# Norms, routing and part of the sends of a routed stage put into the last steps of the cross attention before it

## The reference, cut

```python
x = x + jnp.tanh(g_xattn[2]) * _L2_xattn_ref(_layernorm(x, axis=-1), ctx_1024, ctx_1024, ..., 1)
x = x + jnp.tanh(g_ffn[2]) * _L2_ffn_ref(_layernorm(x, axis=-1), L2_ffn_Wr, L2_ffn_W1, L2_ffn_W2)
```

```python
router_logits = x @ Wr.T                     # 2048 rows, 8 experts
routing_weights = jax.nn.softmax(router_logits, axis=-1)
top_w, top_idx = jax.lax.top_k(routing_weights, TOP_K)      # 2
h = jax.nn.silu(jnp.einsum('td,edf->tef', x, W1))           # 512 hidden
y = jnp.einsum('tef,efd->ted', h, W2)
out = jnp.einsum('te,ted->td', comb, y)
```

## Time and profile before

| | us |
|---|---|
| median of 3 runs | 1419.97 |
| lowest and highest | 1415.36, 1420.51 |
| the profiled execution | 1427.67 |
| its span, first to last instruction | 1425.7 |
| TensorE busy | 1133.1 (79%) |
| VectorE busy | 697.3 (49%) |
| ScalarE busy | 614.2 (43%) |
| GpSimd busy | 443.4 (31%) |

### The profile page before, as it was taken

The page is one execution under the profiler, slowest core; times in us unless marked ns, Lnnn a source line. Parts: engine busy times, 40 slices in busy tenths (PEclk is TensorE's granted clock), DMA queues, the critical chain, the costliest instruction groups (busy, mean ns, idle before and its releaser), DMA issues. The chain is left out here.

```text
span 1425.7 us, 26533 instructions
## 1 busy us (share of the span) xinstructions
PE 1133.1 (79%) x8710; PEld 774.7 (54%) x8710; DVE 697.3 (49%) x3353; ACT 614.2 (43%) x1535; POOL 443.4 (31%) x636
## 2 busy tenths in 40 slices
PE   5998885499989999988987963997586999961684
PEld 3676744277745666653434742786452454441573
DVE  4564546133368776534553452111756788754002
ACT  3454453233369766423213230332462666630453
POOL 1674415333406455400002416343010000016343
PEclk8999987699999999999996865799685899975797
DMA  7499131222069920013530021454143222040343
GB/s 203 131 276 234 38 104 38 60 83 81 22 111 135 170 64 2 2 50 81 100 74 1 2 67 46 144 174 136 36 135 111 69 54 71 20 141 25 97 124 93
DMA packets 150262, 128.54 MB, mean 90 GB/s; under 512 B 13193, under 2 KB 126745, under 8 KB 150136
## 3 DMA queue, kind: packets, MB, share of 16 engines
q1 hardware_dynamic: 135256, 107.67, 31.4%
q0 software_dynamic: 7824, 15.47, 3.9%
q10 hardware_dynamic: 7056, 3.81, 1.0%
HBM read 88.91 MB, written 40.85 MB: 91 GB/s over the span
## 5 line engine op out<-in xcount | busy, mean ns | idle before, releaser
L304 POOL TENSOR_TENSOR L_Z<-L_Z,L_mx 128x512 f32<-128x512 f32 x84 | 88.5, 1055 | 271.1 <-DVE L_mx L615 271.1
L3070 DVE CUSTOM_DVE_ANT_0 L3s_masked<-L3s_psS,L3s_trilw 128x512 f32<-128x512 f32 (+3 forms) x256 | 109.1, 487 | 35.0 <-PE L3s_psS L2969 34.5
L863 ACT ACTIVATE L_Z<-L_Z,L_nmx 128x154 f32<-128x154 f32 x256 | 105.1, 414 | 42.0 <-DVE L_nmx L913 41.9
L3041 ACT ACTIVATE L3s_E<-L3s_psT 128x512 f32<-128x512 f32 (+1 forms) x192 | 87.9, 531 | 49.8 <-PE L3s_psT L2982 49.5
L732 POOL TENSOR_TENSOR L_Z<-L_Z,L_rin 128x488 f32<-128x488 f32 x64 | 64.0, 1000 | 111.8 <-DVE L_rin L921 111.8
L615 DVE CUSTOM_DVE_ANT_0 L_Z<-L_psS,L_Z 128x154 f32<-128x154 f32 x256 | 63.4, 313 | 57.6 <-PE L_psS L352 45.9
L774 PE MATMUL L_psS<-L1k_G,L_xnT 128*128 128x462 f32 x192 | 82.4, 525 | 2.8 <-DVE L_nmx L913 1.4
L913 DVE CUSTOM_DVE_ANT_0 L_Z<-L_psS,L_mask 128x154 f32<-128x154 f32 x256 | 67.7, 313 | 11.2 <-PE L_psS L774 10.7
L513 ACT ACTIVATE L_E<-L_psT 128x512 f32<-128x512 f32 x84 | 46.1, 596 | 57.2 <-PE L_psT L365 57.2
L2969 PE MATMUL L3s_psS<-L3s_KS,L3s_QS 72*128 72x512 bf16 (+3 forms) x256 | 55.9, 336 | 11.4 <-PEq L2955 8.5
L931 DVE COPY L_PT<-L_psT 122x512 f32<-122x512 f32 x64 | 43.6, 682 | 40.4 <-PE L_psT L784 39.5
(11 more groups left out here) (543 smaller groups left out, 2857.5 us busy)
## 6 DMA issues: line engine op xcount, KB each, us to landing
L_Z<-in_fside_Bx16xSxS SPq DMA_DIRECT2D x16, 1232.0 KB
L2f_w<-in_L_ffn_W SPq DMA_DIRECT2D x39, 256.0 KB
slotsL<-empty SPq DMA_DIRECT2D x1, 8320.5 KB, 68.4
L1m_cb<-comb_rows SPq DMA_DIRECT2D x8, 1024.0 KB
L3f_w<-in_L_ffn_fc_w SPq DMA_DIRECT2D x32, 256.0 KB
L0f_w<-in_L_ffn_W SPq DMA_DIRECT2D x24, 256.0 KB
q_parts<-L3s_parts SPq DMA_DIRECT2D x12, 384.0 KB, 5.3
L3s_QS<-q_parts SPq DMA_DIRECT2D x16, 288.0 KB
```

Source lines behind the costliest of these rows:

```text
L304: nc.gpsimd.tensor_tensor(Z[:, t % NZ, h, 0:KM_], Z[:, t % NZ, h, 0:KM_], top.broadcast_to([P, HG, KM_]), ALU.subtract).then_inc(z_ready, 1)
L863: last = nc.scalar.activation(Z[:, t % 2, h], Z[:, t % 2, h], ACT.Exp, scale=-1.0, bias=nmx[:, t % 2, h:h + 1], accum_out=sums[:, t % 2, h ...
L3041: nc.scalar.activation(E[:, g.par, h, EO[group[0]]:EO[group[0]] + wd], psT[:, k, 0:wd], ACT.Exp).then_inc(t_free, 1)
L3070: last = nc.vector.tensor_tensor_reduce(masked[:, k, at:at + wd], psS[:, k, at:at + wd], trilw[:, S - wd:S], 1.0, LOW, ALU.add, ALU.max, m ...
```

## The change

- **Chunks** of L2f are now tile i of every batch (`tiles(k)` is `slice(k, NT, TB)`). So chunks 0, 1 and 2 are the uniform tiles, final after t = 2 of the attention, and chunk 3 is the four tiles of its steps t = 3 to 6.
- **The route is made before the attention** and is handed to both stages; its semaphores live on, and `Keys3` and `SelfState` get their memory earlier too. `begin` moves to the attention's start.
- **In the attention at t = 2**, VectorE measures chunks 0 and 1 between the two residuals, and normalises both and measures chunk 2 behind the second. ScalarE takes the two deviations between its exponentials.
- **At t = 3** TensorE turns chunk 0 and 1 in two new fillings of `psT`, and multiplies with the router into spare columns of `psS`, once all maxima are done. VectorE chooses chunk 0 ahead of the residual.
- **At t = 4 and 5** TensorE counts chunk 0 and 1; VectorE places chunk 0 and chooses chunk 1, then places chunk 1 and normalises chunk 2. ScalarE takes the third deviation.
- **GpSimd**, behind its last subtraction, scatters chunk 0 (8 DMAs) and the first tile of chunk 1 (2 DMAs). The other 22 stay in L2f.
- **`Lead2`** keeps chunks 2 and 3.

The core of the diff:

```diff
+            if late:
+                pool.wait_ge(m.wiped, 64)
+                for g, sent in ((0, route.each(0)), (1, route.sent)):
+                    pool.wait_ge(route.slots_ready, g + 1)
+                    pool.wait_ge(route.pay_done, g + 1)
+                    for t in sent:
+                        route.scatter(pool, m.slots["L2"], t)
...
+            def route_logits(k):
+                pe.wait_ge(t_done, slot[("r", k)] + 1)
+                route.logits(pe, k)
...
+                if late and t in (4, 5):
+                    route.positions(pe, t - 4)
...
+                if late and t == 3:
+                    pe.wait_ge(s_done, 4 * NTL)
+                    route_logits(0)
...
+                if late and t == 3:
+                    route_logits(1)
...
+                    if t == 2:
+                        route.deviation(act, 0)
+                        route.deviation(act, 1)
...
+                if late and t == 4:
+                    route.deviation(act, 2)
...
+                    dve.wait_ge(y_done, written[("y", t)] + 1)
+                    route.moments(0, m.X)
+                    route.moments(1, m.X)
                     dve.wait_ge(y_full, written[("y2", t)] + 1)
                     x = by_batch[:, :, 2]
                     nc.vector.scalar_tensor_tensor(x, y, m.gate(c["gate"]), x, ALU.mult, ALU.add).then_inc(y_done, 1)
+                    route.apply(0, m.X)
+                    route.apply(1, m.X)
+                    dve.wait_ge(y_done, written[("y2", t)] + 1)
+                    route.moments(2, m.X)
...
+                if late and t >= 3:
+                    if t in (4, 5):
+                        route.place(t - 4)
+                    if t in (3, 4):
+                        route.choose(t - 3)
+                    if t == 5:
+                        route.apply(2, m.X)
...
     def tiles(self, k):
-        return slice(k * TB, (k + 1) * TB)
+        return slice(k, NT, TB) if self.c["kind"] == "L2" else slice(k * TB, (k + 1) * TB)
...
     def tensor(self, pe):
         route = self.route
-        route.turn(pe, 0)
-        route.logits(pe, 0)
-        for k in range(TB):
-            if k + 1 < TB:
-                route.turn(pe, k + 1)
-                route.logits(pe, k + 1)
-            route.positions(pe, k)
+        route.turn(pe, 2)
+        route.logits(pe, 2)
+        route.turn(pe, 3)
+        route.positions(pe, 2)
+        route.logits(pe, 3)
+        route.positions(pe, 3)
         self.kv.tensor(pe, self.sa)
...
         route, x = self.route, self.m.X
-        route.begin(dve)
+        route.resume(dve)
+        route.moments(3, x)
+        route.choose(2)
+        route.apply(3, x)
+        route.place(2)
         self.kv.vector(dve)
...
-            for g in range(TB):
+            for g in range(1, TB):
                 pool.wait_ge(route.slots_ready, g + 1)
                 pool.wait_ge(route.pay_done, g + 1)
-                for t in range(g * TB, (g + 1) * TB):
...
+                for t in route.each(g):
+                    if g > 1 or t not in route.sent:
+                        route.scatter(pool, slots, t)
```

More of the change, by code:

```diff
@@ L170, in quad_attention @@
 def quad_attention(nc, m, c):
-    nm, late = c["name"], c["late"]
+    nm, late, route = c["name"], c["late"], c.get("route")
     W, DK = 9, 8
@@ L218, in quad_attention @@
                 take(slot, key)
-            for g in (2, 3, 4):
+            for g in (2, 3):
                 take(slot, ("z", t, g))
+            if not late:
+                take(slot, ("z", t, 4))
             for key in extras(t, 1):
                 take(slot, key)
+            if late:
+                take(slot, ("z", t, 4))
         if 0 <= t - 2 < NTL:
@@ L257, in quad_attention @@
         v_clear, vr_full = sem("v_clear"), sem("vr_full")
+        if late:
+            spare = HG * P - 3 * S2
+            assert spare >= (TB + 1) * route.E
+            route.banks(None, psS[:, 3, 3 * S2:512], psS[:, 2, 3 * S2:512])
+            route.sent = route.each(1)[:1]
         block = ctx.enter_context(nc.Block())
@@ L463, in _ @@
                     turn_scores(t, 3)
+                if late:
+                    for key in extras(t, 1):
+                        extra(key)
                 if last_:
@@ L467, in _ @@
                     turn_scores(t, 4)
-                for key in extras(t, 1):
-                    extra(key)
+                if late and t == 3:
+                    route_logits(1)
+                if not late:
+                    for key in extras(t, 1):
+                        extra(key)
         @block.scalar
@@ L1283, in turn, with turn_rows @@
     def turn(self, pe, k):
+        if k > self.first:
+            pe.wait_ge(self.t_done, k - self.first)
+        self.turn_rows(pe, k, self.bank_t).then_inc(self.t_full, 1)
+    def turn_rows(self, pe, k, bank):
         pe.wait_ge(self.x_ready, k + 1)
-        if k >= 1:
-            pe.wait_ge(self.t_done, k)
-        for i in range(TB):
-            last = pe.transpose(self.bank_t[:, i * P:(i + 1) * P], self.pay[:, 0, k * TB + i, 0:D], self.m.ident)
-        last.then_inc(self.t_full, 1)
+        for i, t in enumerate(self.each(k)):
+            last = pe.transpose(bank[:, i * P:(i + 1) * P], self.pay[:, 0, t, 0:D], self.m.ident)
+        return last
     def logits(self, pe, k):
         E = self.E
-        pe.wait_ge(self.t_done, k + 1)
+        if k >= self.first:
+            pe.wait_ge(self.t_done, k + 1 - self.first)
         if k >= 1:
@@ L1379, in apply @@
         self.dve.wait_ge(self.var_ready, k + 1)
-        for t in range(k * TB, (k + 1) * TB):
+        for t in self.each(k):
             last = nc.vector.tensor_scalar(self.pay[:, 0, t, 0:D], src[:, t], self.mv[:, t, 0:1], self.rs[:, t:t + 1],
@@ L1394, in choose @@
         dve.wait_ge(self.l_free, k + 1)
-        for i in range(TB):
-            own.done(nc.vector.max(self.top8[:, k * TB + i], self.L[:, i]))
+        for i, t in enumerate(self.each(k)):
+            own.done(nc.vector.max(self.top8[:, t], self.L[:, i]))
         own.wait()
-        for i in range(TB):
-            own.done(nc.vector.max_index(self.at8[:, i], self.top8[:, k * TB + i], self.L[:, i]))
+        for i, t in enumerate(self.each(k)):
+            own.done(nc.vector.max_index(self.at8[:, i], self.top8[:, t], self.L[:, i]))
         own.wait()
@@ L1468, in send, with scatter @@
         nc.vector.tensor_tensor(m.slot_to[:, :, ts], r[:, :, ts], z[:], ALU.add).then_inc(self.slots_ready, 1)
+    def scatter(self, pool, slots, t):
+        for k in range(2):
+            pool.indirect_dma_start(slots, bass.IndirectOffsetOnAxis(ap=self.m.slot_to[:, k, t:t + 1], axis=0), self.pay[:, k, t],
+                                    None, bounds_check=slots.shape[0] - 1, oob_is_err=False).then_inc(self.m.scattered, 16)
     def keep_seconds(self):
```

97 lines of the change are left out of this document (54 added, 43 removed).

## The result

| | before | after |
|---|---|---|
| median (7 runs of each) | 1419.03 us | 1403.41 us |
| lowest and highest | 1415.36, 1420.51 | 1398.76, 1410.45 |
| the profiled execution | 1427.67 | 1403.85 |
| its span | 1425.7 | 1402.0 |
| mean granted clock | 0.866 | 0.874 |

The ratio is 0.9895, 95% interval 0.9873 to 0.9917: 14.9 us less, between 12 and 18. The forecast was 1404.0 us, 16 less.

The account below looks back on a forecast made before the run. SyncE's row loads, waiting for all 32 scatters, set the second routed stage's end. Lead 28.1 us shorter minus attention 6.3 longer gives 21.8; allowing for late signals and clock, 13 to 18, taken as 16: 1404 us, range 1396 to 1416.

Follow-up runs that it names:

- R: Not a run but the experiments' measure: time from the attention's residual of tile 2 to SyncE's first row load in the second routed stage; 64.0 us in after.

## What to carry to other kernels

- A barrier behind DMAs that GpSimd issues opens about 2 us later than behind an ordinary instruction; move only so many ahead of it that the last one ends 2 us before the other engines do.
- Work that hands over often between engines was lengthened by scatters beside it in some sets of runs. A move that takes 17 us out of a path by putting transfers beside a tight chain of hand-overs gave 15 us (12 to 18) in one set and 10 (7 to 14) in another. The two intervals overlap, but by R the gain was 17.2 and 6.2, so measure such a move in several sets, on several chips.
- Price the granted clock with any new wait ahead of dense matmuls. The same TensorE code kept the higher clock in four profiles and lost it behind the same 0.90 us in seven; one profile would have shown only one of the two.
- If one profile is 0.5% above its own median, look for the waits that it alone has, before its rows are taken as prices.

## What was not expected of the hardware

- The kernel before takes 1416 to 1419 us in three sets of runs and 1431 to 1434 in two others. The sets were on different chips, as far as the chips are known. The profiles of the two slower sets show waits for TensorE that end 5 to 11 us late while GpSimd's scatters run, at the same places where a kernel was profiled twice, with lengths that go with the set.
- In the loop over blocks SyncE's loads, each with an address that it reads into a register, start 1.1 us apart (876.30, 877.41, 878.50 in after). Two for each block are 2.2 us, where TensorE, with rows at hand, needed 1.9 for its nine matmuls; the queue of an engine that computes nothing was the bound of a stage of 86 us.
